# The graph stage of a four-layer graph network, spread over the dense stages of layers 0 and 1

## What is computed

```
h = relu(layernorm(x));  x = x + h @ M          # M: 256 x 256, a product of plane rotations (src, dst, edge_weight)
h = relu(layernorm(x));  x = x + attention_1(h, edges, attributes)   # q, k, v and skip: h @ [256 x 1024]
h = relu(layernorm(x));  x = x + gat_2(h, edges)
h = relu(layernorm(x));  x = x + gat_3(h, edges, attributes)
```

## Time and profile before

| | us |
|---|---|
| median of 3 runs | 3290.62 (3285.22 to 3292.22) |
| the profiled execution: its own time | 3284.5 |
| the profiled execution: its span | 3282.7 |
| granted TensorE clock, mean over the span | 0.861 of 2.4 GHz |
| PE busy, share of the span | 2532.6, 77% |
| DVE busy | 2318.6, 71% |
| ACT busy | 1697.1, 52% |
| POOL busy | 1516.0, 46% |

### The profile page before, as it was taken

The page is one execution under the profiler, slowest core; times in us unless marked ns, Lnnn a source line. Parts: engine busy times, 40 slices in busy tenths (PEclk is TensorE's granted clock), DMA queues, the critical chain, the costliest instruction groups (busy, mean ns, idle before and its releaser), DMA issues. The chain is left out here.

```text
span 3282.7 us, 56360 instructions
## 1 busy us (share of the span) xinstructions
PE 2532.6 (77%) x12612; PEld 1931.7 (59%) x12613; DVE 2318.6 (71%) x5874; ACT 1697.1 (52%) x4048; POOL 1516.0 (46%) x1759
## 2 busy tenths in 40 slices
PE   2999998457999999999994478888870578788870
PEld 1888887323666666666663356666650466666650
DVE  4888887474787878778785367766778456666667
ACT  1666665212555555555552366666651366666651
POOL 1333332102454455554540277777740277777740
PEclk9999999778999999999997677777885778787785
DMA  2100000314566566656650355555522355555521
GB/s 68 23 10 8 10 8 9 65 54 128 150 161 164 160 165 162 161 162 166 161 153 16 99 139 138 137 139 138 137 64 38 108 142 142 141 141 141 140 64 39
DMA packets 186288, 348.93 MB, mean 106 GB/s; under 512 B 74085, under 2 KB 116478, under 8 KB 185951
## 3 DMA queue, kind: packets, MB, share of 16 engines
q0 software_dynamic: 83520, 249.39, 29.9%
q1 hardware_dynamic: 102685, 98.62, 10.5%
HBM read 325.45 MB, written 22.44 MB: 106 GB/s over the span
## 5 line engine op out<-in xcount | busy, mean ns | idle before, releaser
L1689 POOL DMA_INDIRECT t_rows<-table_h,t_istage x896 | 854.3, 953 | 266.2 <-issue 249.2
L1776 PE MATMUL t_pso<-t_rows,t_hot 125*125 125x272 f32 (+1 forms) x1792 | 603.1, 493 | 71.8 <-DVE t_rows L1815 36.5
L1265 POOL DMA_INDIRECT b_rows<-table_kv,b_istage x448 | 457.8, 1022 | 380.6 <-PE b_pso L1401 257.7
L1776 PEld LDWEIGHTS t_pso<-t_rows,t_hot 125*125 125x125 f32 x1792 | 405.8, 238 | 171.6 <-issue 71.8
L1327 ACT COPY b_asked<-b_psq 125x512 f32<-125x512 f32 x224 | 131.1, 585 | 428.0 <-PE b_psq L1366 428.0
L1815 DVE TENSOR_TENSOR t_rows<-t_rows,t_psm 125x1056 f32<-125x1056 f32 x224 | 276.8, 1236 | 33.4 <-issue 33.2
L1762 PE MATMUL t_pss<-node_scores,t_hot_t 125*125 x1792 | 270.6, 281 | 33.0 <-ACT t_hot_t L1720 30.4
L1762 PEld LDWEIGHTS t_pss<-node_scores,t_hot_t 125*125 125x125 f32 x1792 | 265.0, 228 | 48.7 <-issue 43.5
L1727 ACT ACTIVATE t_hot<-con_iota,g_dstl 125x125 f32<-125x125 f32 x896 | 280.3, 384 | 0.0
L1825 DVE TENSOR_TENSOR acc<-acc,t_pso 125x272 f32 (+1 forms) x448 | 192.7, 430 | 123.4 <-DVE acc L1825 71.2
L1366 PE MATMUL b_psq<-queries,b_hot_t 125*125 x896 | 237.1, 388 | 40.2 <-issue 24.4
(11 more groups left out here) (395 smaller groups left out, 4970.2 us busy)
## 6 DMA issues: line engine op xcount, KB each, us to landing
t_places<-targets SPq DMA_DIRECT2D x56, 488.3 KB
t_rows<-table_h,t_istage POOLq DMA_INDIRECT x896, 3.3
b_attr<-in_attr_t SPq DMA_DIRECT2D x224, 62.5 KB
b_places<-targets SPq DMA_DIRECT2D x28, 488.3 KB
b_rows<-table_kv,b_istage POOLq DMA_INDIRECT x448, 5.4
table_h<-d_stage SPq DMA_DIRECT2D x50, 132.8 KB
t_flag<-flags SPq DMA_DIRECT2D x56, 62.5 KB
table_kv<-d_moved SPq DMA_DIRECT2D x25, 128.9 KB
```

The lines of the kernel that those rows point to most:

```text
L1265: pool.indirect_dma_start(out=rows[:, h, s, :], out_offset=None, in_=table, in_offset=bass.IndirectOffsetOnAxis(ap=istage[:, h, s:s + 1], ...
L1689: pool.indirect_dma_start(out=rows[:, r, s, :], out_offset=None, in_=table, in_offset=bass.IndirectOffsetOnAxis(ap=istage[:, r, s:s + 1], ...
L1776: mm = pe.matmul(ps_o[b % 2][0:P, at:at + mw], hot[:, r, b * G + u, :], rows[0:P, r, b * G + u, 0:mw], start=u % PAIR == 0, stop=u % PAIR ...
```

## The change

The graph stage is gone. `graph_phase` becomes `graph_work`, a set of pieces for each engine, which opens no stage of its own:
- **In layer 0's dense stage** each engine's queue takes the pieces in. DVE: *compare* between `measure(0)` and `level(0)`; *choose* before `finish(0, 0)`; after the five tiles of group 0 *stairs*, of group 1 *fold*, of group 2 *live*, of group 3 *close*, of group 4 *columns*. PE: the 5 counting products ahead of group 0, the 12 transposes between groups 3 and 4. POOL and SP, idle in this stage before, take their queues from the graph stage (without the borders and without the loads of layer 1). Here the groups are written out five times and not as a loop.
- **In layer 1's dense stage** SP first issues the four loads of layer 1 and then the 8 and 2 reads of the borders. DVE waits for the loads ahead of group 0, PE ahead of its first product. In group 0 DVE does the three instructions of the flags one each after `finish(0, 1)`, `(0, 2)` and `(0, 3)`, and the lanes after `finish(0, 4)`. SP writes `flags` and `lanes` behind the last tile's store, and the stage ends when they have landed.
- **The lanes** are made on 28 partitions (one for each chunk) without the eightfold copy by heads: a memset of 34 values, 2 comparisons of 16, one multiplication of 34; the store repeats them for the 8 heads (2 transfers of 28 x 8 runs of 34 bytes).
- In all dense stages PE's last group is written out of the loop (`tapered` for `peeled`).

What is computed in each piece is the same. The diff, cut to its core:

```diff
-def graph_phase(nc, con, g, src2, dst2, dst_e, live, targets, lanes, flags, loads, a, w):
+def graph_work(nc, ph, con, g, src2, dst2, dst_e, live, targets, a, w):
...
-        near = sb("g_near", [128, CHUNKS, P + 2])
-        flag = sb("g_flags", [128, CHUNKS, 2, P], BF16)
-        sides = sb("g_sides", [1, 2, STEPS + 1])
-        lane = sb("g_lanes", [1, 2, CHUNKS, H, LANE], BF16)
...
-        loads = loads + [(att[n][:], a[n].to_broadcast([128, D])) for n in att] + [...]
+    loads = [(att[n][:], a[n].to_broadcast([128, D])) for n in att] + [(wedge[0:ED], a["we3"]), (wedge[ED:], a["we3"])]
...
-                dve.wait_ge(sideset, 32)
-                c.then(dve.memset(lane[:], 1.0))
-                for a in range(2):
-                    now, prior = (sides[:, a, k:k + STEPS]...)
-                    for h in range(H):
-                        c.up(dve.tensor_tensor(lane[:, a, :, h, 1:LANE], now, prior, ALU.not_equal))
-                dve.wait_ge(dv, c.n)
-                dve.tensor_scalar(lane[:], lane[:], -BIG, None, ALU.mult).then_inc(laned, 1)
...
 def dense_phase(..., graph=None, borders=None):
...
+        work = graph(ph) if graph else None
+        early = layer == 1
+        if borders:
+            live, lanes, flags = borders
+            near, flag = sb("near", [128, CHUNKS, P + 2]), sb("flags", [128, CHUNKS, 2, P], BF16)
+            sides, lane = sb("sides", [CHUNKS, 2, RUN + 1]), sb("lanes", [CHUNKS, 2, LANE], BF16)
+        def run(eng, body):
+            if work:
+                for i in range(GROUPS):
+                    body(i)
+            else:
+                tapered(eng, GROUPS, body)
...
+                def fences(k):
+                    if k < 2:
+                        if k == 0:
+                            dve.wait_ge(nearset, 16 * H)
+                        ends = near[:, :, 2 * k:P + 2 * k]
+                        dve.tensor_tensor(flag[:, :, k], near[...], ends[...], ALU.not_equal).then_inc(flagged, 1)
+                    else:
+                        dve.wait_ge(flagged, 2)
+                        dve.tensor_scalar(flag[:], flag[:], -BIG, None, ALU.mult).then_inc(flagged, 1)
+                def rails():
+                    dve.memset(lane[:], 1.0).then_inc(laned, 1)
+                    dve.wait_ge(sideset, 32)
+                    dve.wait_ge(laned, 1)
+                    for k in range(2):
+                        now, prior = (sides[:, k, x:x + RUN][:, ::-1 if k else 1] for x in (1, 0))
+                        dve.tensor_tensor(lane[:, k, 1:LANE], now, prior, ALU.not_equal).then_inc(laned, 1)
+                    dve.wait_ge(laned, 3)
+                    dve.tensor_scalar(lane[:], lane[:], -BIG, None, ALU.mult).then_inc(laned, 1)
                 def body(i):
                     if not last(i):
                         measure(i + 1)
+                    if work and i == 0:
+                        work.choose(dve, gc)
                     finish(i, 0)
                     if not last(i):
                         level(i + 1)
                     for u in range(1, U):
                         finish(i, u)
+                        if borders and opening(i):
+                            if u < U - 1:
+                                fences(u - 1)
+                            else:
+                                rails()
+                    if work:
+                        if i == 0:
+                            work.stairs(dve, gc)
+                        elif i == 1:
+                            work.fold(dve, gc)
+                        elif i == 2:
+                            work.live(dve, gc)
+                        elif i == 3:
+                            work.close(dve, gc)
+                        else:
+                            work.columns(dve, gc)
...
                 measure(0)
+                if work:
+                    gc = work.tally(dve)
+                    work.compare(dve, gc)
                 level(0)
-                tapered(dve, GROUPS, body)
+                if early:
+                    dve.wait_ge(brought, 16 * len(loads))
+                run(dve, body)
...
                 def multiply(i, u):
                     n = i * U + u
                     pe.wait_ge(tcopied, n + 1)
-                    if u >= 3 or not isinstance(i, int):
+                    if u >= 3 or not opening(i):
                         pe.wait_ge(evac, n - 2 if u >= 3 else n - 1)
+                    if early and opening(i) and u == 0:
+                        pe.wait_ge(brought, 16 * len(loads))
...
                     multiply(i, U - 1)
-                peeled(pe, GROUPS, body)
+                    if work and i == 3:
+                        work.turn(pe)
+                if work:
+                    work.count(pe)
+                run(pe, body)
...
                     for to, at in loads:
                         sp.dma_start(to, at).then_inc(brought, 16)
+                    if borders:
+                        around = bass.AP(live.tensor, live.offset, [[P, RUN], [RUN * P, CHUNKS], [1, P + 2]])
+                        for h in range(H):
+                            sp.dma_start(near[h:128 - H + h + 1:H], around).then_inc(nearset, 16)
+                        for k in range(2):
+                            ends = bass.AP(live.tensor, live.offset + k, [[RUN * P, CHUNKS], [P, RUN + 1], [1, 1]])
+                            sp.dma_start(sides[:, k]..., ends, ...).then_inc(sideset, 16)
...
                     peeled(sp, GROUPS, body)
+                    if borders:
+                        sp.wait_ge(flagged, 3)
+                        sp.dma_start(flags, flag[:].rearrange("q c a e -> q (c a e)")).then_inc(marked, 16)
+                        sp.wait_ge(laned, 4)
+                        for k in range(2):
+                            sp.dma_start(lanes[k:k + 1]..., lane[:, k].unsqueeze(1).to_broadcast([CHUNKS, H, LANE])).then_inc(marked, 16)
+                        sp.wait_ge(marked, 48)
...
-            dense_phase(nc, con, 0, X, None, None, MT, ROT, None, [])
+            dense_phase(nc, con, 0, X, None, None, MT, ROT, None, [],
+                        graph=lambda ph: graph_work(nc, ph, con, g, ..., live, targets, a, w))
...
-                graph_phase(nc, con, g, ..., live, targets, lanes, flags, loads, a, w)
-                dense_phase(nc, con, 1, X, acc, asks, w1, 4 * D, b1, [t1])
+                dense_phase(nc, con, 1, X, acc, asks, w1, 4 * D, b1, [t1], loads=loads, borders=(live, lanes, flags))
```

More of the change, by code:

```diff
@@ L921, in dense_phase @@
+def dense_phase(nc, con, layer, X, acc, ntab, weight, width, bias, tables, base=None, settle=False, loads=(), graph=None, borders=None):
     U = 5
@@ L1009, in finish @@
                                         o[:, 0:D].rearrange("p (h c) -> p h c", h=H)).then_inc(evac, 1)
+                def fences(k):
[3 more added lines that the diff above has]
+                        ends = near[:, :, 2 * k:P + 2 * k]
+                        dve.tensor_tensor(flag[:, :, k], near[:, :, 1:P + 1][:, :, ::-1 if k else 1], ends[:, :, ::-1 if k else 1], ALU.not_equal).then_inc(flagged, 1)
+                    else:
[10 more added lines that the diff above has]
+                    dve.tensor_scalar(lane[:], lane[:], -BIG, None, ALU.mult).then_inc(laned, 1)
                 def body(i):
@@ L1033, in _ @@
                     dve.scalar_tensor_tensor(ntab[:, :, H:2 * H], ntab[:, :, H:2 * H], 0.2, ntab[:, :, H:2 * H], ALU.mult, ALU.max).then_inc(slanted, 1)
+            if work:
+                block.gpsimd(work.gpsimd)
+                block.sync(work.sync)
             if layer:
@@ L1074, in _ @@
                     act.wait_ge(empty, 1)
-                tapered(act, GROUPS, body)
+                run(act, body)
             @block.tensor
@@ L1081, in turn @@
                     pe.wait_ge(hset, n + 1)
-                    if u >= 2 or not isinstance(i, int):
+                    if u >= 2 or not opening(i):
                         pe.wait_ge(tcopied, n if u == 0 else n - 1)
@@ L2092, in program @@
         later += [(w[k][:, :, 0:D], rows(a[n]), con["w_brought"]) for k, n in (("l2", "w2"), ("l3", "w3"))]
+        g = {"srcs": sb("g_srcs", [ROWS, STEPS], I32), "dstl": sb("g_dstl", [P, STEPS]), "closing": sb("g_closing", [P, STEPS]),
+             "stairs": sb("g_stairs", [1, WORDS], I32)}
+        rows2 = lambda x: x.rearrange("(k p) -> k p", p=P)
+        live = nc.dram_tensor("live_targets", (STEPS * P + 2,), F32, kind="Internal").ap()
+        targets = nc.dram_tensor("targets", (1, STEPS * P), BF16, kind="Internal").ap()
         with ExitStack() as lists:
@@ L2098, in program @@
             rotation_phase(nc, con, fields, prefixes, ends, MT, later)
-            dense_phase(nc, con, 0, X, None, None, MT, ROT, None, [])
+            dense_phase(nc, con, 0, X, None, None, MT, ROT, None, [],
+                        graph=lambda ph: graph_work(nc, ph, con, g, rows2(a["src"]), rows2(a["dst"]), a["dst_e"], live, targets, a, w))
```

(5 more changed lines are left out.)

291 lines of the change are left out of this document (143 added, 148 removed).

## The result

The changed kernel takes 3248.57 us (median of 4 runs, 3243.90 to 3255.69) where the kernel before, on the same chip, takes 3289.81: a ratio of 0.9877, with a 95% interval from 0.9863 to 0.9891. The forecast was 3248.5. The profiled execution took 3248.09 (span 3246.0). As will be seen, the total is nearer than the steps that led to it.

What follows compares the result with a forecast made beforehand. Stages stand one behind another with barriers, so each counts whole: -75.3 for the graph stage, +22.5 in layer 0, +10.7 in layer 1 make -42.1 us, from 3290.6 to 3248.5; range 3239 to 3261.

Steps and rivals of the forecast that it cites:

- Layer 0, +22.5: Layer 0's dense stage: the graph work taken in, slow clock included, lengthens it by 22.5 us, from 43.5 to 66.
- the ring: Layer 0's dense stage: engines wait on each other in a circle, so DVE work at a group's end adds its whole length.
- Close* and the turns: Layer 0, between groups 3 and 4: DVE's close and PE's 12 transposes add 2.4 us, bounds 1.6 and 3.2.
- The clock: Layer 0: PE idles behind fold and live, falls to 1.2 GHz, tiles 2 to 4 of groups 2 and 3 slow: +4.3 us.
- The groups without a loop: Layer 0's dense stage: groups written out make measure and level faster, 0.5 us for each of three groups: -1.5 us.
- Layer 1, +6.0: Layer 1's dense stage lengthens by 6.0 us: 1.3 for bare loads, 4.7 for DVE's flags work making PE late.
- the loads, +1.3: Layer 1's start: loads, now bare, arrive 7.7 us after the stage's start; PE's first product, before at 6.38, is 1.3 later.
- Rival 4: Layer 1: loads and borders' reads delay one another by 6 us, DVE holds up PE; 3254 to 3258 us; chance 0.08.
- The end, +4.7: Behind layer 1's last store: the flags' write is bare for 4.7 us, the lanes' transfers cost nothing; bounds 3.5 and 7.
- Rival 2: Layer 0: transposes before group 4 let the clock fall, slowing its five tiles; 3252 us, 3254.5 with dear lanes; chance 0.18.
- Rival 3: More is hidden: clock stays up after live or fold, PE's lead in layer 1 larger, flags leave sooner; 3241.3 us; chance 0.17.
- rival 5: Layer 1 stays at 1.2 GHz after PE's pauses; slower than before, 3340 us with all 25 tiles slow; chance 0.02.

Runs made afterwards that it cites:

- experiment 6: Changed kernel with fold's nine products moved behind close and its sums spread between group 4's additions; layer 0's dense stage 58.65 us for 65.44.
- experiment 1: Changed kernel with SP waiting for layer 1's four loads before issuing the borders' reads; layer 1's dense stage 113.7 us for 116.1.
- Experiment 5: Changed kernel with layer 1's four loads issued in layer 0's dense stage, behind those of fold; layer 1's dense stage 107.90 us, 8.2 less.
- experiments 1 and 2: The run holding the borders' reads back (113.7 us), and the changed kernel with b1 spread to 128 partitions, not 125 (110.3); layer 1's dense stage was 116.1.
- experiment 3: Changed kernel with SP writing flags and lanes behind group 0's stores, not the last tile's; layer 1's dense stage 116.00 us for 116.13.
- the three edits: Changed kernel with flags written early, fold spread over group 4 and layer 1's loads issued in layer 0; 3227.22 us, 0.9810 of the kernel before.

## Why the prediction was right, and where it was not

**Layer 0, +22.5, measured +21.96.** *Stairs* 2.4, *fold* 6.1, *live* 4.7 and *columns* 1.6 stand whole in the stage, as the ring said; that *fold* was dear only for its place is shown by experiment 6. Group 0 ended 3.5 later, for 2.4. *Close* and the turns cost 1.1 for 2.4: the turns ran at full clock, in 2.0 us (622.09 to 624.05) instead of 3.2. The clock cost more than the 4.3: from the second addition to the last it is 4.77, 4.89 and 5.08 us in groups 1, 2 and 3, where a group at full clock has 3.08, together +5.5. Groups 2 and 3, for which it was foreseen, have 3.8 of it; the 1.7 of group 1 were not foreseen, because with *stairs* a pause of up to 3.8 us was taken to be too short for the clock to fall. The groups without a loop gave 2.9 for 1.5: from a group's last addition to the next group's second it is, without the work put in between, 3.67 us for 4.84, of which 0.2 come back behind it. Group 0 and the clock were put 2.3 us too low, the turns and the loops 2.7 too high, and so the sum is nearer than its terms.

**Layer 1, +6.0, measured +12.5: the step that failed is "the loads, +1.3".** It took the arrival from one row of the graph stage and put the reads behind them at no price. That row shows how many bytes moved in 7.5 us (245 GB/s, 1.84 MB), not which: loads issued behind `b1` were among them. Another half megabyte moved by 622, and the earlier trace rows has the engines at 0.38 and 134 GB/s from 619.90 to 622.15, near the pace that `b1` has by itself in experiment 1. So the kernel before does not show that `b1` was in after 7.5 us, and nobody waited for it there. In the changed kernel it came 11.5 us after its issue. With the first eight products, which now ran at half clock for longer and took 6.54 us for 5.29, this term is 6.80 + 1.25 = 8.05. Experiment 5 takes 8.2 away by removing these transfers; experiments 1 and 2 give its parts: 2.5 for the reads, up to 5.9 for the 125 rows (together a little more than the whole, so they overlap). Rival 4 had that mechanism, with 0.08 and 6 us, but on `near`, which in truth nobody waited for. The flags cost 4.4 for 4.7, and PE's pause of 2.3 us ahead of `multiply(1, 2)` is where it was said to be.

**The end, +4.7, measured +6.4.** The lanes' transfers were put at nothing. Their issue took 2.5 us, but it was over at 752.65, while `flags` still moved:

```profile
749.73 0.37 SPq L1189 DMA_DIRECT2D flags<-d_flags  x1
750.16 2.49 SPq L1192 DMA_DIRECT2D lanes<-d_lanes  x2
```

```profile
751.00:755.00 4.00, 0.00 (x0) 0.00 (x0) 0.00 (x0) 0.00 (x0) 0.00 (x0) 0.50 1.01 407
757.00:760.20 3.20, 0.00 (x0) 0.00 (x0) 0.00 (x0) 0.00 (x0) 0.00 (x0) 0.50 0.00 0
```

The last bytes moved 7.6 us behind the start of this stretch, for 3.0 before: that is about the 4.7. The other 1.8 are time in which nothing moves, 3.5 us for 1.6 before. With the writes issued early it is 1.7 again (experiment 3), so it belongs to them; what passes in it no run shows.

**Why the total was right nevertheless.** That it came within 0.1 us is luck. The steps were some 8 us too kind (6.5 in layer 1, 1.7 at the end, less 0.5 in layer 0). From the profiled execution they gave 3242.4, and that execution took 3248.1. The stages behind, unchanged, took 2.7 less, and the forecast was set on a median that stood 6.1 above the profile of before, where that of the changed kernel stands 0.5 above its own. These two make up for the 8, and neither was reasoned about. The medians on chip C also fall by more than the stages do: 39.4 for 35.2, and 62.1 for 54.7 with the three edits. Since only one profile of before exists on a chip of that speed, and the 2488 us of stages behind scatter by some microseconds, the remainder stays open.

**The signs.** Of what was to show it, the length of layer 0's stage came (65.4 for 66), `measure` at 2.8, the clock of 0.50 with the slow tiles (2 us apart, not 1.8) and the pause of 2.3 us; the first product (13.2 for 7.7), layer 1's length (116.1 for 109.6) and the end (11.1 for 9.4) did not. None of the three signs of a wrong forecast came: DVE did not wait for `near`, layer 0's stage grew by 22, and no later stage changed its length by more than 1.6 us. They did not cover the step that failed.

**The rivals.** Rival 2 (the turns let the clock fall) did not happen: the clock was 1.00 from 622 to 630. The Trainium skill, page "TensorE: Matmul & The Clock Gate", section "Part 4: PE-mode transpose", says that a transpose does not count as PE-busy in the same way. The trace neither bears that out nor refutes it: the turns were 2.0 us, and no run here makes them longer. Rival 3 fell with the slow tiles, rival 5 with a clock of 0.93 in layer 1.

## What to carry to other kernels

When a stage that hid transfers is dissolved, go through each transfer that it issued for the next one and ask where it can be issued now; here they were the dearest term, and issuing them a stage earlier gave 8 us back. Work put between the steps of a ring costs its whole length plus the slow clock behind it, while the same work placed where the engine was waiting anyway cost 0.5 us of its 6.1. Bytes moved in a stretch do not say which transfer has landed; where nobody waits for one, its arrival has to be bounded and not read off. A total that agrees is no proof of its terms: compare stage by stage.

## What the hardware showed beyond expectation

- A load spread to 125 partitions kept 0.32 of the 16 DMA engines busy, at 116 GB/s; the same values to 128 partitions released PE 6.7 us after their issue instead of 11.6.
- The issue of eight reads on SP's queue took 13.2 us behind two larger loads and 5.3 to 5.6 with these landed first or gone (experiments 1 and 5): a long issue here meant that transfers ahead were still under way.
- The clock fell to 0.50 behind a pause of 2.27 us, and at a moment when PE had been at work again for 1.2 us; with *fold* spread out it fell at about 588.3, behind a pause of 2.89 us that had ended at 587.59.
- The kernel before took 3289, 3617 and 3640 us on three chips; between its profile on the first chip and that on B, 331 of 336 us lie behind the start of the blend. A gain of 13 us in one stage that one chip's time shows (0.9952) another's does not (0.9999).
